# Between two transformer layers: zeros of two operand stacks written by ScalarE, the first head chunk of layer 1 placed by token half, its first maxima ordered by query tile

## The chip, the cores and the metric

One core of one Trainium2 chip. The metric is the device time of one execution in microseconds (us), lower is better. Engines are named as in the profile: PE (TensorE matmul), PEld (its weight loads), DVE (VectorE), ACT (ScalarE), POOL (GpSimd), SP (SyncE, which here only issues DMAs; SPq is its queue).

## The reference, cut to what matters

A two-layer block network over 1024 tokens (a 32 x 32 grid) of 384 channels, everything in float32:

```
x = x + attention0(ln(x))      # 12 heads of 32, full 1024 x 1024, relative positions
t = t + moe0(ln(t))            # 8 experts, 2 per token
x = x + attention1(ln(x))      # 12 query heads, 4 key/value heads, 7 x 7 neighbourhood
t = t + moe1(ln(t))            # 8 experts, 2 per token, and one shared expert
```

The change lies at the seam: the end of `moe0`, where each token gathers its two expert rows and adds them, and the start of `attention1`. In `attention1` the scores are `q k / sqrt(32)` inside the 7 x 7 window, a softmax over the window, and the weighted sum of values.

## The kernel before, in words

**Tiling.** The tokens stand in 8 tiles of 128 (`NT`), two halves of 4 tiles (`HALF`, 512 tokens each). The 12 query heads stand in 3 chunks of 4 (`KC` chunks, `G` heads). One core runs both layers in turn; each engine has its own program (`@block.sync`, `gpsimd`, `scalar`, `vector`, `tensor`), and they meet only in semaphores.

**End of layer 0.** The routed experts work on 23 blocks of 128 rows. When the last block's result is copied out of PSUM (`y_dve` reaches `ROUTED_BLOCKS`) SP stores it to DRAM (L602). POOL then gathers two rows per token, one tile at a time: 16 indirect DMAs (L880), two per tile, the tiles 4 to 7 only after the tile four (one less) before them has been added. DVE adds the two rows with their weights (L1367, L1369) and takes the statistics of the next layer norm (L1114). After four tiles DVE and ACT normalise the half (ACT's square root is L893), and PE transposes it (L1422).

**Start of layer 1.** PE transposes half 0, runs the four projection jobs of half 0 (keys, then the queries of the three chunks; L1397), transposes half 1 and runs the same four jobs for half 1. Each job is rounded by ACT into a high part (L923, L932) and its remainder taken by DVE as a low part (L1135), which raises `job_dve`. ACT and DVE copy the transposes of half 1 before they take the first job of half 0, because that is their program order.

**The stacks.** A score matmul contracts over 128 partitions: for each head the operand `QA` (queries) holds 32 rows of the high query part, 64 rows of mask, and the high part again; `KS` (keys) holds high keys, 64 rows of position keys and low keys; `QB` holds low queries, 32 rows that later take the row maxima, and 64 rows of zeros (partitions 64 to 127). The stacks of layer 1 lie in memory that layer 0's expert weights used, so they can be written only when the experts are done, except for `QA` and `KS` of stack 0, whose mask and position rows are placed during the experts. SP places `QA` and `QB` rows by SBUF-to-SBUF DMAs (`place`, L543), one per head and 32 rows; POOL places the keys (L777). Before, SP issued at the end of layer 0 three transfers of 1 MB each out of DRAM: zeros for `QB` of stack 0, mask for `QA` of stack 1, zeros for `QB` of stack 1. Then it waited for chunk 0's queries of both halves:

```
sp.wait_ge(job_dve, job_number(1, "q", 0))
stack_direct(0)                      # 8 DMAs into QA, 4 into QB, 128 KB each
sp.wait_ge(job_dve, job_number(1, "q", 2))
stack_direct(1)                      # the same for chunk 1
```

**First maxima.** The softmax subtracts a row maximum that is found ahead of the scores: PE makes the high-part scores of one head and one query tile (`max_piece`, L1471), DVE reduces them (L1156). The work goes in six blocks, chunk by chunk, half by half. The first block has 16 pieces (4 heads x the 4 query tiles of half 0), and nothing to run beside it but the 8 value projections (L1451), one after each second piece. A query tile needs the keys of its own tile and of one on each side. `tile_of` sets the order: head by head, four query tiles each. PE turns the maxima into rows (`maxima_rows`, L1485), ACT copies them into `QB` (`copy_rows`, L946), and the scores (L1501, L1503), exponentials (L962) and weighted sums (L1520, L1531) follow. The pieces of block n+1 go between the scores of block n. PE waited for all of `QA` of chunk 0 and all keys before the first piece:

```
pe.wait_ge(a_in[0], placed(A_DMAS, layer, 0))
pe.wait_ge(k_in[layer], 16 * K_DMAS)
for i in range(TILES):
    max_piece(first_block, i)
```

Of the kernel before, what the change touches and what calls it, by code (L numbers as in the profile page):

```python
# [41 lines left out]
P = 128  # L42
# [55 lines left out]
def build(nc, x, qkv_w, qk_b, v_b, proj_w, proj_b, rel_both, Wr0, br0, Wgu0, bgu0, Wd0, bd0,  # L98
# [17 lines left out]
    with ctx:  # L116
        def sem(name):
            return ctx.enter_context(nc.semaphore(name))
# [137 lines left out]
        zero_rows = nc.dram_tensor("zero_rows", [2 * D, T], F32, kind="Internal").ap()  # L256
# [34 lines left out]
        k_stored = sem("k_stored")  # L291
        a_in = [sem("a_in0"), sem("a_in1")]
# [63 lines left out]
        A_DMAS = [[17, 7, 6], [10, 9, 8]]  # L356
        B_DMAS = [[16, 4, 4], [5, 5, 4]]
# [120 lines left out]

        def tile_of(hb, j):

            return hb // HALF % KC, j // (NT // HALF), hb % HALF * (NT // HALF) + j % (NT // HALF)
# [37 lines left out]
        def _(sp):  # L519
# [37 lines left out]
            def place_same(dst, rows, done):  # L557

                place(dst, rows.rearrange("p (a t) -> p a t", a=1).broadcast_to([rows.shape[0], G, T]), done)
# [85 lines left out]
            for n in range(2):  # L645
                sp.dma_start(zero_rows[D * n:D * n + D, :], mask_const[0:D, :]).then_inc(const_stored, 16)
# [12 lines left out]
            sp.wait_ge(const_stored, 16 * 6)  # L659
            sp.wait_ge(proj_dve, NT)  # L660
            sp.dma_start(Wqkv[1][:, :, :], w_qkv1.rearrange("(k p) n -> p k n", p=P)).then_inc(wq_in[1], 16)
            place_same(KS[1][0][D:3 * D], key_rows[1], a_in[0])
            place_same(QA[1][0][D:3 * D], mask_rows, a_in[0])
            routed(0)

            place_same(QB[1][0][2 * D:P], zero_rows, b_in[0])
            place_same(QA[1][1][D:3 * D], mask_rows, a_in[1])
            place_same(QB[1][1][2 * D:P], zero_rows, b_in[1])
# [8 lines left out]
            sp.wait_ge(job_dve, job_number(1, "q", 0))  # L677
            stack_direct(0)
            check(a_in[0], A_DMAS[1][0])
            check(b_in[0], B_DMAS[1][0])  # L680
            sp.wait_ge(job_dve, job_number(1, "q", 2))
# [19 lines left out]
        def _(pool):  # L701
# [58 lines left out]
            for layer in range(2):  # L760
# [11 lines left out]
                if layer:  # L772

                    pool.wait_ge(job_dve, job_number(1, "k", 0))
                    for dst, src in ((KS[1][0][0:D], k_part(1, 0, False)), (KS[1][0][3 * D:P], k_part(1, 0, True))):
                        for g in range(G):
                            pool.dma_start(dst[:, g, :].bitcast(F32), src[D * g:D * g + D].bitcast(F32)).then_inc(k_in[1], 16)  # L777
# [108 lines left out]
        def _(act):  # L886
# [22 lines left out]
            for layer in range(2):  # L909
                ln_and_transposes(2 * layer)  # L910
# [27 lines left out]
                def copy_rows(c, half, pair):  # L938

                    hb = BLOCKS * layer + HALF * c + half  # L940
                    if pair == 0:
                        act.wait_ge(nmax_psum, hb + 1)
                        act.wait_ge(b_in[c % 2], placed(B_DMAS, layer, c))
                    rows = 1 if layer == 0 else D
                    for g in (2 * pair, 2 * pair + 1):
                        last = act.activation(QB[layer][c % 2][D:D + rows, g, half * BANK:(half + 1) * BANK],  # L946
                                              PS[D * g:D * g + rows, 4, :], ACT.Copy)
                    last.then_inc(nmax_act, 1)
# [431 lines left out]
        def _(pe):  # L1380
# [55 lines left out]
            for layer in range(2):  # L1436
# [116 lines left out]
                pe.wait_ge(a_in[0], placed(A_DMAS, layer, 0))  # L1553
                pe.wait_ge(k_in[layer], 16 * K_DMAS)
                first_block = BLOCKS * layer
                for i in range(TILES):
                    max_piece(first_block, i)
                    if i % 2 == 1:
                        values(i // 2)
# [6 lines left out]
                for c in range(KC):  # L1566
                    for u in range(U[layer]):
# [5 lines left out]
                        if some and some[0] == 0 and half == 1:  # L1573
                            pe.wait_ge(a_in[(c + 1) % 2], placed(A_DMAS, layer, c + 1))

# [174 lines left out]
```

## Time and profile before

| what | value |
|---|---|
| three runs | 1140.9, 1142.8, 1146.92 us, median 1142.8 |
| the profiled execution | 1143.17 us, of which the traced span is 1141.6 us |
| mean granted TensorE clock | 0.958 of full speed |
| busy share of the span | PE 89%, PEld 51%, DVE 45%, ACT 28%, POOL 28% |
| the seam, from the last expert store to the first score of layer 1 | 538.6 to 611.4 us of the span |

Times in rows are microseconds from the start of the span, ns where that is written. A timeline row is: start, duration, engine, line, operation, what is written and read, count, and in brackets the idle time of the engine ahead of it with what ended it. A row of several instructions (xN) is merged. Full speed of the clock is 2.4 GHz, its other level 1.2 GHz.

### The profile page before, as it was taken

To read this page: it belongs to the slowest core of one execution; us is meant where nothing else is said; L and a number is where in the kernel's file an instruction comes from. 1 tells how busy PE (TensorE), PEld (TensorE's weight loads), DVE (VectorE), ACT (ScalarE), POOL (GpSimd) and SP (SyncE) were. 2 spreads that over 40 slices of the span, in tenths; PEclk is the share of its full clock that TensorE was granted. 3 is DMA by queue.
4 is the path that set the end of the run, shared out by engine and by line. 5 is a ranking of instruction groups with operands and counts; after the bars stand their busy time and mean duration, and the time that the engine had idled before them with its cause. 6 is when DMAs were issued, how large, how long until landed. Compare 5 with 4: busy or idle time off the path is not lost.

```text
span 1141.6 us, 13662 instructions
## 1 busy us (share of the span) xinstructions
PE 1011.7 (89%) x4561; PEld 587.9 (51%) x4562; DVE 510.3 (45%) x898; ACT 321.9 (28%) x492; POOL 323.9 (28%) x281
## 2 busy tenths in 40 slices
PE   6999999999980799997278888979999999999998
PEld 3755555554440466664136656558554554455554
DVE  4566687888562255553534465671111111111114
ACT  3514544554611122121014545241111111111100
POOL 5514677777735001000510000254000000000004
PEclk9999999999995799999598999999999999999999
DMA  8599308000077236411733100523344424411005
GB/s 293 148 284 279 85 14 172 1 1 1 2 269 260 70 138 221 152 55 50 206 96 73 43 15 2 193 78 118 131 152 160 158 81 175 175 51 42 14 27 159
DMA packets 47114, 132.45 MB, mean 116 GB/s; under 512 B 6865, under 2 KB 25817, under 8 KB 46808
## 3 DMA queue, kind: packets, MB, share of 16 engines
q1 hardware_dynamic: 32424, 67.41, 20.4%
q0 software_dynamic: 14640, 64.36, 15.8%
q8 instruction: 32, 0.52, 0.2%
q14 instruction: 18, 0.15, 0.0%
HBM read 89.88 MB, written 30.87 MB: 106 GB/s over the span
## 4 chain that ended last, share of the span: by engine, by line
PE 71%; DVE 9%; DMA 8%; ACT 5%; issue 4%; POOL 3%; SPq 1%; POOLq 0%; DVEq 0%; ACTq 0%
PE PS L1667 21%; PE PS L1688 10%; PE PS L1471 6%; PE PS L1520 5%; PE PS L1397 5%; PE PS L1640 4%; DMA Wd<-in_Wd_r 4%; PE PS L1501 3%; DVE nmax_part L1156 3%; PE PS L1503 3%; PE PS L1714 3%; ACT QB L946 2%; DMA bd<-in_bd 2%; PE PS L1451 2%; DVE exp_acc L1188 2%
## 5 line engine op out<-in xcount | busy, mean ns | idle before, releaser
L1667 PE MATMUL PS<-Wgu,xbT 128*128 x690 | 285.5, 556 | 9.2 <-DMA Wd<-in_Wd_r 5.4
L1667 PEld LDWEIGHTS PS<-Wgu,xbT 128*128 128x128 f32 x690 | 127.9, 191 | 127.6 <-issue 114.8
L962 ACT ACTIVATE expS<-PS 128x1024 f32<-128x1024 f32 (+3 forms) x156 | 135.5, 878 | 135.2 <-PE PS L1503 134.0
L1688 PE MATMUL PS<-Wd,hidT 128*128 x414 | 143.1, 491 | 1.5 <-DVE hidT L1297 0.8
L798 POOL TENSOR_TENSOR exp_acc<-exp_acc,expS 128x512 f32<-128x512 f32 (+1 forms) x65 | 124.5, 1915 | 47.6 <-ACT expS L962 46.8
L1471 PE MATMUL PS<-KS,QA 128*128 128x512 f32 (+2 forms) x288 | 109.3, 426 | 18.7 <-DVE nmax L1156 6.8
L1501 PE MATMUL PS<-QA,KS 128*128 128x512 f32 (+3 forms) x312 | 116.9, 380 | 9.0 <-ACT QB L946 9.0
L1156 DVE TENSOR_REDUCE nmax_part<-PS 128x1 f32<-128x512 f32 x160 | 103.6, 684 | 46.0 <-PE PS L1471 45.2
L1503 PE MATMUL PS<-QB,KS 128*128 128x512 f32 (+3 forms) x312 | 111.7, 364 | 0.0
L1688 PEld LDWEIGHTS PS<-Wd,hidT 128*128 128x128 f32 x414 | 78.7, 191 | 57.6 <-issue 14.4
L1471 PEld LDWEIGHTS PS<-KS,QA 128*128 128x128 f32 x288 | 52.2, 191 | 83.1 <-DVE nmax_part L1156 44.6
L1071 ACT ACTIVATE hidT<-PS 128x384 f32<-128x384 f32 x46 | 22.6, 491 | 253.2 <-PE PS L1676 253.2
L1156 DVE TENSOR_REDUCE nmax<-PS 128x1 f32<-128x384 f32 (+2 forms) x112 | 66.4, 621 | 59.1 <-PE PS L1471 57.9
L880 POOL DMA_INDIRECT got<-block_rows_out,row_i x32 | 30.8, 963 | 211.7 <-DMA block_rows_out<-yb 199.8
L1501 PEld LDWEIGHTS PS<-QA,KS 128*128 128x128 f32 x312 | 59.9, 192 | 39.8 <-ACT QB L946 18.2
L1520 PE MATMUL PS<-expS,V 128*32 128x512 f32 (+3 forms) x624 | 71.6, 531 | 0.1
L1297 DVE COPY hidT<-PS 128x384 f32<-128x384 f32 x23 | 12.8, 558 | 120.1 <-PE PS L1676 120.0
L1503 PEld LDWEIGHTS PS<-QB,KS 128*128 128x128 f32 x312 | 60.1, 193 | 7.3
L1397 PE MATMUL PS<-XnT,Wqkv 128*128 128x512 f32 x120 | 56.9, 634 | 3.4 <-issue 2.0
L826 POOL DMA_DIRECT2D Wgu<-in_Wg_r x8 | 6.0, 755 | 189.2 <-DVE yb L1335 167.0
L1306 DVE TENSOR_TENSOR hid<-gated,PS 128x768 f32<-128x768 f32 x23 | 21.9, 954 | 79.8 <-ACT gated L1063 79.8
L1313 DVE TENSOR_TENSOR pre<-PS,bgu 128x768 f32<-128x768 f32 x23 | 22.0, 957 | 78.9 <-PE PS L1667 72.8
(170 smaller groups left out, 1177.2 us busy)
## 6 DMA issues: line engine op xcount, KB each, us to landing
Wgu<-in_Wgu POOLq DMA_DIRECT2D x8, 1152.0 KB, 6.3
Wgu<-in_Wg_r POOLq DMA_DIRECT2D x8, 1152.0 KB, 6.4
Wgu<-in_Wu_r POOLq DMA_DIRECT2D x8, 1152.0 KB, 8.5
Wd<-in_Wd_r POOLq DMA_DIRECT2D x8, 1152.0 KB, 10.8
xb<-block_rows_in SPq DMA_DIRECT2D x46, 192.0 KB, 2.4
block_rows_out<-yb SPq DMA_DIRECT2D x46, 192.0 KB, 1.9
part_rows<-parts SPq DMA_DIRECT2D x2, 3072.0 KB, 17.9
Wd<-in_Wd POOLq DMA_DIRECT2D x8, 576.0 KB, 7.1
```

The source lines that it names most:

```text
L798: last = pool.tensor_tensor(acc, older, exp_tile(0, c, u)[:, pair, heads], ALU.add)
L962: act.activation(exp_tile(layer, c, unit)[:, pair, :].rearrange("p (b n) -> p b n", b=2)[:, :, lo:hi], PS[:, 2 * pair:2 * pair + 2, lo:hi] ...
L1156: dve.tensor_reduce(dst, src, axis=AX.XY if hb == 0 else AX.X, op=ALU.max, negate=True).then_inc(max_done, 1)
L1397: last = pe.matmul(PS[:, bank, :], Wqkv[layer][:, kc, col:col + P], XnT[:, kc, b * BANK:(b + 1) * BANK], start=kc == 0, stop=kc == KC - 1)
L1471: last = pe.matmul(PS[:, bank + (k - lo) // BANK, 0:n], QA[layer][c % 2][:, g, qt * P:(qt + 1) * P], KS[layer][c % 2][:, g, k:k + n], star ...
L1501: pe.matmul(PS[:, 2 * pair + j, lo:hi], keys, QA[layer][c % 2][:, g, queries], start=True, stop=False)
L1503: last = pe.matmul(PS[:, 2 * pair + j, lo:hi], keys, QB[layer][c % 2][:, g, queries], start=False, stop=True)
L1520: last = pe.matmul(PS[D * g:D * g + D, 6, lo:hi], V[:, kt, vcol:vcol + D], probabilities(c, u, g), start=first, stop=last_one, skip_group_ ...
L1640: last = pe.matmul(PS[:, 2 * (n % 3) + up, :], w, rows, start=i == 0, stop=i == len(products) - 1)
L1667: last = pe.matmul(PS[:, 3 * par + lo // BANK, 0:n], xbT[:, par, kc, :], Wgu[layer][:, bass.ds(s, 1), kc, lo:lo + n], start=kc == 0, stop= ...
L1688: last = pe.matmul(PS[:, 7, 0:C], hidT[layer][:, par, i, :], Wd[layer][:, bass.ds(s, 1), i, :], start=i == 0, stop=i == m.IC - 1)
L1714: last = pe.matmul(PS[:, 3 + t % 3, 0:C], shared_hidT[:, f, t * P:(t + 1) * P], shared_d[:, f, :], start=f == 0, stop=f == m.IC - 1)
```

## The change

ScalarE writes the zero rows of both `QB` stacks, as soon as the last expert block is copied out, with two activations of 64 x 4096 elements (`Copy`, scale 0). The two 1 MB zero loads, their DRAM tensor and the two stores that filled it go away. The 1 MB mask load for `QA` of stack 1 is issued by SP after chunk 0's queries. Chunk 0's queries and the keys are placed in two token halves, so with twice as many DMAs of half the size (64 KB): half 0 when the first two jobs (SP) or the first job (POOL) are done, half 1 after jobs 6 and 5. The first block's pieces go query tile by query tile, four heads each; the first 12 need only half 0, the last 4 also the keys of half 1. PE waits for the early semaphores in front of the first piece, for half 1's keys in front of piece 12, and for half 1's queries in front of the second block's first piece. ACT waits for the early `QB` rows in front of the first `copy_rows`.

```diff
--- before.py
+++ after.py
@@ -253,7 +253,6 @@
         ys = nc.dram_tensor("block_rows_out", [ROUTED_BLOCKS * P, C], F32, kind="Internal").ap()
 
         key_rows = [nc.dram_tensor(f"key_rows{n}", [2 * D, T], F32, kind="Internal").ap() for n in range(2)]
-        zero_rows = nc.dram_tensor("zero_rows", [2 * D, T], F32, kind="Internal").ap()
         mask_rows = nc.dram_tensor("mask_rows", [2 * D, T], F32, kind="Internal").ap()
 
 
@@ -289,6 +288,10 @@
         hi_act = sem("hi_act")
         parts_stored = sem("parts_stored")
         k_stored = sem("k_stored")
+        a_early = sem("a_early")
+        b_early = sem("b_early")
+        k_early = sem("k_early")
+        fixed_in = sem("fixed_in")
         a_in = [sem("a_in0"), sem("a_in1")]
         b_in = [sem("b_in0"), sem("b_in1")]
         v_psum = sem("v_psum")
@@ -353,8 +356,8 @@
         block = ctx.enter_context(nc.Block())
 
 
-        A_DMAS = [[17, 7, 6], [10, 9, 8]]
-        B_DMAS = [[16, 4, 4], [5, 5, 4]]
+        A_DMAS = [[17, 7, 6], [8, 9, 8]]
+        B_DMAS = [[16, 4, 4], [4, 4, 4]]
 
         W_LOAD = [16 * 4, 16 * 3]
         W_BEFORE = [0, E * W_LOAD[0]]
@@ -476,8 +479,12 @@
 
             return (BLOCKS - 1 + TAIL_CUTS) * (hb // BLOCKS) + hb % BLOCKS
 
+        EARLY_TILES = (NT // HALF - 1) * G
+
         def tile_of(hb, j):
 
+            if hb == BLOCKS:
+                return 0, j % G, j // G
             return hb // HALF % KC, j // (NT // HALF), hb % HALF * (NT // HALF) + j % (NT // HALF)
 
         def piece_place(hb, i):
@@ -642,8 +649,6 @@
 
             sp.wait_ge(pool_const, 3)
             sp.dma_start(mask_rows[:, :], mask_const[D:3 * D, :]).then_inc(const_stored, 16)
-            for n in range(2):
-                sp.dma_start(zero_rows[D * n:D * n + D, :], mask_const[0:D, :]).then_inc(const_stored, 16)
 
             sp.wait_ge(k_stored, 16 * 2)
             sp.wait_ge(parts_stored, 16 * PARTS_STORED)
@@ -656,16 +661,12 @@
             stack_from_rows(2)
 
 
-            sp.wait_ge(const_stored, 16 * 6)
+            sp.wait_ge(const_stored, 16 * 4)
             sp.wait_ge(proj_dve, NT)
             sp.dma_start(Wqkv[1][:, :, :], w_qkv1.rearrange("(k p) n -> p k n", p=P)).then_inc(wq_in[1], 16)
-            place_same(KS[1][0][D:3 * D], key_rows[1], a_in[0])
-            place_same(QA[1][0][D:3 * D], mask_rows, a_in[0])
+            place_same(KS[1][0][D:3 * D], key_rows[1], fixed_in)
+            place_same(QA[1][0][D:3 * D], mask_rows, fixed_in)
             routed(0)
-
-            place_same(QB[1][0][2 * D:P], zero_rows, b_in[0])
-            place_same(QA[1][1][D:3 * D], mask_rows, a_in[1])
-            place_same(QB[1][1][2 * D:P], zero_rows, b_in[1])
 
             def stack_direct(c):
 
@@ -674,10 +675,21 @@
                     place_direct(QA[1][s][lo:lo + D], q_part(1, c, False), "qk", a_in[s])
                 place_direct(QB[1][s][0:D], q_part(1, c, True), "qk", b_in[s])
 
-            sp.wait_ge(job_dve, job_number(1, "q", 0))
-            stack_direct(0)
+            for half in range(HALF):
+                cols = slice(half * BANK, (half + 1) * BANK)
+                done_a, done_b = (a_early, b_early) if half == 0 else (a_in[0], b_in[0])
+                sp.wait_ge(job_dve, JOBS[0] + JOBS[1] // HALF * half + 2)
+                for lo in (0, D * 3):
+                    for g in range(G):
+                        place(QA[1][0][lo:lo + D, g, cols], q_part(1, 0, False)[D * g:D * g + D, cols].bitcast(F32), done_a)
+                for g in range(G):
+                    place(QB[1][0][0:D, g, cols], q_part(1, 0, True)[D * g:D * g + D, cols].bitcast(F32), done_b)
+            check(fixed_in, 2)
+            check(a_early, 2 * G)
+            check(b_early, G)
             check(a_in[0], A_DMAS[1][0])
             check(b_in[0], B_DMAS[1][0])
+            place_same(QA[1][1][D:3 * D], mask_rows, a_in[1])
             sp.wait_ge(job_dve, job_number(1, "q", 2))
             stack_direct(1)
             check(a_in[1], A_DMAS[1][1])
@@ -771,10 +783,13 @@
 
                 if layer:
 
-                    pool.wait_ge(job_dve, job_number(1, "k", 0))
-                    for dst, src in ((KS[1][0][0:D], k_part(1, 0, False)), (KS[1][0][3 * D:P], k_part(1, 0, True))):
-                        for g in range(G):
-                            pool.dma_start(dst[:, g, :].bitcast(F32), src[D * g:D * g + D].bitcast(F32)).then_inc(k_in[1], 16)
+                    for half in range(HALF):
+                        cols = slice(half * BANK, (half + 1) * BANK)
+                        pool.wait_ge(job_dve, JOBS[0] + JOBS[1] // HALF * half + 1)
+                        for dst, src in ((KS[1][0][0:D], k_part(1, 0, False)), (KS[1][0][3 * D:P], k_part(1, 0, True))):
+                            for g in range(G):
+                                pool.dma_start(dst[:, g, cols].bitcast(F32),
+                                               src[D * g:D * g + D, cols].bitcast(F32)).then_inc(k_in[1] if half else k_early, 16)
 
                 def accumulate(hb, v):
 
@@ -907,6 +922,12 @@
                 copy(1, 0)
 
             for layer in range(2):
+                if layer:
+
+                    act.wait_ge(y_dve, ROUTED_BLOCKS)
+                    for low in QB[1]:
+                        act.activation(low[2 * D:P, :, :].rearrange("p g t -> p (g t)"),
+                                       ones[2 * D:P, 0:1].broadcast_to([2 * D, G * T]), ACT.Copy, scale=0.0)
                 ln_and_transposes(2 * layer)
                 if layer == 0:
                     act.wait_ge(qk_bias_in, 16)
@@ -940,7 +961,10 @@
                     hb = BLOCKS * layer + HALF * c + half
                     if pair == 0:
                         act.wait_ge(nmax_psum, hb + 1)
-                        act.wait_ge(b_in[c % 2], placed(B_DMAS, layer, c))
+                        if hb == BLOCKS:
+                            act.wait_ge(b_early, 16 * G)
+                        else:
+                            act.wait_ge(b_in[c % 2], placed(B_DMAS, layer, c))
                     rows = 1 if layer == 0 else D
                     for g in (2 * pair, 2 * pair + 1):
                         last = act.activation(QB[layer][c % 2][D:D + rows, g, half * BANK:(half + 1) * BANK],
@@ -1550,10 +1574,16 @@
                     last.then_inc(sums_psum, 1)
 
 
-                pe.wait_ge(a_in[0], placed(A_DMAS, layer, 0))
-                pe.wait_ge(k_in[layer], 16 * K_DMAS)
+                if layer:
+                    pe.wait_ge(fixed_in, 16 * 2)
+                    pe.wait_ge(a_early, 16 * 2 * G)
+                    pe.wait_ge(k_early, 16 * K_DMAS)
                 first_block = BLOCKS * layer
                 for i in range(TILES):
+                    if layer == 0 and i == 0:
+                        pe.wait_ge(a_in[0], placed(A_DMAS, 0, 0))
+                    if i == (EARLY_TILES if layer else 0):
+                        pe.wait_ge(k_in[layer], 16 * K_DMAS)
                     max_piece(first_block, i)
                     if i % 2 == 1:
                         values(i // 2)
@@ -1572,6 +1602,8 @@
                         per = 2 if layer == 0 else 1
                         if some and some[0] == 0 and half == 1:
                             pe.wait_ge(a_in[(c + 1) % 2], placed(A_DMAS, layer, c + 1))
+                        if some and some[0] == 0 and layer and c == half == 0:
+                            pe.wait_ge(a_in[0], placed(A_DMAS, 1, 0))
 
 
                         after = (c, u + 1) if u + 1 < U[layer] else (c + 1, 0)
```

## Rows read from the trace of the kernel before

**Rows 1.** Chain of waits over the whole span, shares by engine (the page, part 4)

```profile
PE 71%; DVE 9%; DMA 8%; ACT 5%; issue 4%; POOL 3%; SPq 1%; POOLq 0%; DVEq 0%; ACTq 0%
```

**Rows 2.** Chain of waits, 536 to 615 us: start, duration, what

```profile
547.01 9.94 DMA got<-block_rows_out,row_i
...
562.33 3.36 PE PS L1422 x12
...
566.36 13.21 PE PS L1397 x24
...
591.01 1.48 SPq L543
...
594.47 3.36 DMA QA<-q_part
...
608.62 1.28 ACT L987
...
610.12 0.59 ACT QB L946
```

**Rows 3.** Timeline, 537 to 562 us

```profile
538.94 0.66 SPq L543 DMA_DIRECT2D QB<-zero_rows  x1
...
549.51 0.95 POOL L880 DMA_INDIRECT got<-block_rows_out,row_i  x1 [0.30 <-issue]
...
558.76 0.60 DVE L1367 SCALAR_TENSOR_TENSOR X<-got,weight,X 128x384 f32<-128x384 f32 x1
...
561.26 0.20 ACT L893 ACTIVATE std<-var_eps 128x4 f32<-128x4 f32 x1 [26.28 <-DVE var_eps L1099]
```

**Rows 4.** The one gather (L880) that starts in 558 to 559 us

```profile
L880 POOL DMA_INDIRECT got<-block_rows_out,row_i x1: 947/947/947, 558.5 to 558.5; - x1
...
DMA to landing us min/median/max: 3.1/3.1/3.1
```

**Rows 5.** The 16 gathers of layer 1 (L880, 1110 to 1130 us), issue to landing

```profile
DMA to landing us min/median/max: 2.9/3.6/4.6
```

**Rows 6.** The three 1 MB transfers (L543, 535 to 545 us), issue to landing

```profile
DMA to landing us min/median/max: 7.7/11.0/17.5
```

**Rows 7.** Busy time in stretches: length, engines' busy (count), PE clock, DMA share, GB/s

```profile
544.00:550.00 6.00, 0.00 (x0) 0.00 (x0) 0.00 (x0) 0.00 (x0) 4.48 (x6) 0.50 1.01 325
...
566.30:571.60 5.30, 5.24 (x6) 2.18 (x7) 4.76 (x14) 0.21 (x2) 0.00 (x0) 0.50 0.01 3
...
592.40:598.00 5.60, 0.01 (x1) 0.00 (x0) 0.69 (x1) 0.60 (x1) 0.00 (x0) 0.79 0.92 244
598.00:602.50 4.50, 4.43 (x19) 4.47 (x20) 2.02 (x5) 0.56 (x2) 0.00 (x0) 0.51 0.93 203
...
612.50:616.10 3.60, 3.52 (x13) 3.52 (x13) 0.56 (x1) 2.04 (x4) 0.00 (x0) 0.53 0.02 5
```

**Rows 8.** ScalarE by shape: the longest plain activation

```profile
L962 ACT ACTIVATE expS<-PS 128x1024 f32<-128x1024 f32 x96 | 97.7, 1026 | 86.9 <-PE PS L1503 86.6
```

**Rows 9.** Timeline, 580 to 600 us: low parts of the jobs and placements

```profile
582.29 1.87 DVE L1135 SCALAR_TENSOR_TENSOR q_part<-PS,q_part 128x512 fp32r<-128x512 f32 x3
...
586.34 4.01 POOL L777 DMA_DIRECT2D KS<-k_part  x8 [22.78 <-DVE k_part L1135]
...
588.65 6.41 SPq L543 DMA_DIRECT2D QA<-q_part  x8
...
593.08 0.69 DVE L1135 SCALAR_TENSOR_TENSOR q_part<-PS,q_part 128x512 fp32r<-128x512 f32 x1 [1.88 <-ACT q_part L923]
```

**Rows 10.** The reductions of the first block (L1156, 590 to 612 us)

```profile
L1156 DVE TENSOR_REDUCE nmax<-PS x16: 424/547/558, 598.7 to 607.9; 128x1 f32<-128x384 f32 x12, 128x1 f32<-128x256 f32 x4
```

**Rows 11.** Timeline of PE: first piece, maxima rows of block 1, first piece of chunk 1

```profile
598.07 0.87 PE L1471 MATMUL PS<-KS,QA 128*128 128x256 f32 x2 [5.65 <-DMA QA<-q_part]
...
608.55 1.08 PE L1485 MATMUL PS<-ident,nmax 128*32 128x128 f32 x32 [0.27 <-DVE nmax L1156]
...
634.40 0.28 PE L1471 MATMUL PS<-KS,QA 128*128 128x256 f32 x1
```


## The prediction

> **What bounds the kernel now.** I read the page's chain first: PE carries 71% of it and DMA 8% [rows 1], so time off PE is worth looking for only where PE stands still. The chain between 536 and 615 us shows two such places at the seam.
>
> *Place A, the combine.* Before PE can transpose half 0 of layer 1's input at 562.33, the chain sits 9.94 us in one gather that POOL issued at 547.01 [rows 2]. The timeline shows what else was in flight: SP issued the first of its three 1 MB transfers at 538.94, just ahead of the gathers [rows 3]. They took 7.7 to 17.5 us to land [rows 6], and in 544 to 550 the DMA engines were busy for the whole stretch (share 1.01) while no compute engine but POOL, which issues the gathers, did anything [rows 7]. A gather issued at 558.5, when the three had landed, took 3.1 us [rows 4]; the 16 gathers of layer 1, without such company, took 2.9 to 4.6 [rows 5].
>
> *Place B, the placement.* The last low part of the jobs ends at 593.08 + 0.69 = 593.77 [rows 9]. The first piece of the maxima starts at 598.07, and what it waited for is a `QA` placement [rows 11]. In the chain that is SP's issues, one after the other, and 3.36 us of landing [rows 2]. Then PE's granted clock is at its lower level (0.51) for 598 to 602.5, after a stretch in which PE had done almost nothing [rows 7].
>
> After the seam everything hangs on PE's progress through layer 1: its loads and its stages are released by the attention's own steps, so what is gained ahead of the first scores should reach the end whole.
>
> **Part 1: zeros by ScalarE.** It removes two of the three transfers ahead of the gathers; moving the mask (part 2) removes the third. The last gather of half 0 is the eighth, issued at 549.51 [rows 3]; nothing in its issue waits for DVE, so that time stays. It lands after 3.1 us [rows 4] instead of being served behind 3 MB: 549.51 + 3.1 = 552.6, and the fourth tile's addition, which started at 558.76 [rows 3], starts there: **6.15 us** earlier. (The third tile, issued at 547.01, would be landed by 550.1 and added in time.) From there statistics, normalisation and PE's transposes follow as before: 562.33 becomes 556.2. Bounds: 2.9 and 4.6 us of landing [rows 5] give 6.35 and 4.65.
>
> Half 1 does not become the new bound. POOL no longer waits for DVE, so the sixteenth gather is issued some 8 x 1.25 us after the eighth (POOL's pace between 547.01 and 549.51 [rows 2, 3]), at 559.5, and lands by 562.7; with the 3.6 us from addition to transpose that half 0 takes (558.76 to 562.33), half 1 is ready at 566.3. PE is busy with half 0's jobs until 556.2 plus what it needs now from 562.33 to 579.57 (566.36 + 13.21) [rows 2], so until 573.4: 7 us of cover.
>
> The price on ScalarE: 1024 elements per partition take 1.03 us [rows 8], so 4096 take at most 4.1 and two of them 8.2, from about 538.9 (SP's zero load waits for the same last block [rows 3]) to 547.1. Its next work is the square root, due at 561.26 - 6.15 = 555.1, idle 26 us before it [rows 3]. So they cost nothing, with 8 us of cover, even if a table load of 1.28 us [rows 2] comes behind them. If the cover were gone, each us would delay half 0's normalisation by as much.
>
> PE starts half 0's jobs at the clock's lower level now (0.50 from 566.3 to 571.6 [rows 7]). It has still stood idle for some 18 us before, so I leave that as it is. Reaching the full clock a us sooner or later would be worth about 0.5 us, up or down.
>
> **Part 2: placement by half, and the mask moved.** In this part I keep the trace's own times, without the 6.15. The first two jobs' low parts are there at 582.29 + 1.87/3 = 582.9 [rows 9]. SP then issues eight early `QA` DMAs. Eight took 6.41 us, two long ones among them [rows 9, 2], so the eighth is issued by 588.7 and, with the old landing of 3.36 for twice the bytes, is there at 592.1. POOL's eight early key DMAs take 4.01 us of issue [rows 9]; from 582.9 they are out at 586.9 and, with the slowest landing of rows 5, there by 591.5. Both are ahead of 593.77, when the last low part is ready and PE, which waits for all eight jobs, may go on. So PE's wait changes owner: no longer a DMA, but DVE's last low part. First piece at about **594.0** instead of 598.07: 4.05 us. Cover: 1.7 us; a later landing costs what exceeds it.
>
> Half 1's keys, eight more POOL issues, are out by 591 and there by 595.5; piece 12 comes no sooner than 599. Half 1's queries are the twentieth SP issue: 582.9 + 20 x 0.80 (6.41/8) = 598.9, landing 602.3. PE wants them after the first scores, which wait for ACT's row copies (610.12 now [rows 2], about 604.4 then): 2 us of cover at that slow pace. Behind them in SP's queue stand four `QB` DMAs, the mask and chunk 1's twelve, treated under the rivals.
>
> **Part 3: order of the pieces.** The 16 reductions are the same, 12 x 0.558 + 4 x 0.424 = 8.4 us of DVE [rows 10]. PE's gap in front of them shrinks from 4.3 us to its own wait for DVE, some 1.6 us, so I expect its clock to stay at full speed, and then DVE's rate is the bound: 594.0 + 0.35 to the first output + 8.4 = 602.75, where the rows start at 608.55 today [rows 11]. That is **5.75 us** in all for place B. If the clock falls as it does now, the pace of today stays and B is worth 4.05 (the lower bound). Above it: if the second slow stretch, 612.5 to 616.1 at 0.53 [rows 7], goes as well, half of its 3.6 us, 1.8 more. ACT's table load and row copies follow the last value copy as now and shift with it.
>
> The two dropped stores early in layer 0 and the new semaphore waits have cover of many us and I cost them at nothing.
>
> **Sum.** 6.15 + 5.75 = 11.9 us. The profiled execution took 1143.17 around its span of 1141.6, 0.4 above the median of the three runs; 1143.17 - 11.9 = 1131.3, from the median 1130.9. I say **1131**. The terms' bounds give 4.65 + 4.05 = 8.7 (1134.3) to 6.35 + 5.75 + 1.8 = 13.9 (1129), and with the runs' scatter 1127 to 1135 for this case alone. From no change such a measurement can tell about 0.5%, 5.7 us.
>
> **Rivals.**
> *Only the gathers gain.* The early placement is late or something else holds the first piece: 1143.17 - 6.15 = 1137.0. For it: when POOL and SP placed together, some SP issues took up to 1.48 us [rows 2], and the cover is 1.7 us. Against: half the bytes per DMA. Chance 0.09.
>
> *Only the placement gains.* The gathers are slow by themselves: 1137.4. Against it stand the 3.1 us of a gather after the transfers [rows 4] and layer 1's [rows 5]. Chance 0.05.
>
> *More DMAs eat the gain.* SP issues 24 placements for chunk 0 instead of 12. At 1.48 us each, half 1's queries would land at 582.9 + 29.6 + 3.4 = 615.9, 11.5 late, and nothing is left: 1142.8. Only two issues of the old twelve were so long. Chance 0.07 for this or a like loss.
> The Trainium skill ("DMA: Bandwidth & Descriptors", rules for kernel authors) speaks against this part: it says to coalesce many small transfers, because under 64 KB mostly overhead is paid, and gives about 2 us plus bytes over 436 GB/s for one. By that an estimate is 2.15 us for 64 KB against 2.3 for 128; were the eight early ones served one after another, they would be done at 600.1, B would lose 2 us instead of gaining, and the time would be about 1139. The trace does not agree that they are serial: eight of 128 KB were out in 6.41 us and the last landed 3.36 us after its issue [rows 9, 2].
>
> *Slower: chunk 1 comes late.* The mask, 1 MB, now stands in SP's queue between chunk 0's 24 and chunk 1's 12 placements, and PE wants chunk 1 at 634.40 [rows 11], 628.65 with B's gain. 37 issues at 0.80 end at 612.5; with the slowest landing of a 1 MB transfer, 17.5 [rows 6], that is 630, a loss of 1.4 us only. At 1.1 us per issue with that landing it is 641 and the gain is gone; at 1.25 it is 646.7, 18 late, and the time is 1149. Against: the mask has no other 1 MB transfers and no gathers beside it there. Chance 0.03.
>
> **How the numbers follow.** The forecast has 0.76. The range has to reach to the two half gains, so 1127 to 1137.5. Faster by over 0.5%: 0.76, the 0.09 (6.15 is just over 5.7) and half of the 0.05, so 0.88. Within 0.5%: the rest of that and the 0.07, so 0.09. Slower: 0.03.
>
> **What the changed profile would show.** The gathers L880 of half 0 land in about 3 us and the DMA share ahead of them is well under 1; two ScalarE activations of some 4 us begin right after the last expert block. The chain at the seam goes through POOL's gather issues, not through a 9.9 us DMA. The first piece is released by the last DVE low part, some 0.2 us after it; the clock in that stretch stays near 1. No wait of PE on half 1's queries or on chunk 1. Wrong would be: gathers of 7 us or more; a first piece released by a DMA; a clock of 0.5 under the first maxima; or a gain at the first score that is smaller at the end of the attention.

## The result and the profile after

The changed kernel takes 1135.15 us (median of 8 runs, 1130.58 to 1136.01) against 1143.27 for the kernel before (8 runs, 1140.9 to 1148.52): ratio 0.9911, 95% interval 0.9889 to 0.9933. A second batch of the same kernel gave 1133.27 and the same ratio. 1143.27 x 0.0089 is 10.2 us less, with the interval 7.7 to 12.7; the medians themselves lie 8.1 us apart, in the second batch 9.8. The forecast was 11.9, inside the interval. The profiled execution took 1133.86 us around a span of 1132.3.

The chain of waits of the changed kernel, down to the row copies, answers to [rows 2] (start, duration, what); the last three lines are from later stages:

```profile
550.12 3.00 DMA got<-block_rows_out,row_i
...
556.68 3.37 PE PS L1446 x12
...
560.73 13.04 PE PS L1421 x24
...
587.27 0.70 DVE q_part L1159
...
588.42 0.47 PE PS L1495 x2
...
596.93 1.28 ACT L1011
...
598.44 0.59 ACT QB L970
...
728.55 4.32 PE PS L1455 x6
...
861.65 11.12 DMA Wd<-in_Wd_r
...
872.95 7.08 PE PS L1699 x12
```

The 9.94 us in one gather have become 3.00, the `QA` placement and SP's issues are gone from the chain, and in their place stands DVE's last low part (the line that is left out between the last low part and the first piece is 0.45 us of issue). The first row copy comes at 598.44 instead of 610.12, although the layer before it ended 0.6 us later here (the first gather starts at 541.27 instead of 540.67).

The timeline of the combine answers to [rows 3]; the brackets say how long the engine had been idle and what ended that:

```profile
539.18 7.12 ACT L929 ACTIVATE QB<-ones 64x4096 fp32r<-64x4096 f32 x2 [4.80 <-DVE yb L1361]
...
546.31 1.28 ACT L908 ACT_TABLE_LOAD   x1
...
553.14 0.62 DVE L1391 SCALAR_TENSOR_TENSOR X<-got,weight,X 128x384 f32<-128x384 f32 x1 [0.60 <-DMA got<-block_rows_out,row_i]
...
555.70 0.20 ACT L908 ACTIVATE std<-var_eps 128x4 f32<-128x4 f32 x1 [8.11 <-DVE var_eps L1123]
```

Two zero activations take 7.1 us, 3.6 each, and 8.1 us of cover (idle time of ScalarE before its square root) are left. In 544 to 550 us the DMA share is 0.58 where it was 1.01 [rows 7]. All 16 gathers land in about 3 us now (min, median, max; 3.0, 7.5 and 9.9 before):

```profile
L895 POOL DMA_INDIRECT got<-block_rows_out,row_i x16: 942/946/1316, 541.3 to 560.7; - x16
...
DMA to landing us min/median/max: 3.0/3.0/3.7
```

Around the first maxima the busy time in stretches answers to [rows 7] (length, busy time of PE, PEld, DVE, ACT, POOL, PE clock, DMA share, GB/s). PE's gap is 1.8 us, and the clock stays:

```profile
586.60:588.40 1.80, 0.00 (x0) 0.01 (x1) 0.69 (x1) 0.60 (x1) 0.00 (x0) 1.00 0.44 114
588.40:590.40 2.00, 1.98 (x17) 2.00 (x18) 1.44 (x4) 0.28 (x1) 0.00 (x0) 1.00 0.40 98
590.40:592.40 2.00, 2.00 (x18) 2.00 (x17) 1.79 (x5) 0.56 (x2) 0.00 (x0) 1.00 0.40 98
```

**What the end gets.** The span is 9.3 us shorter, the first row copy 12.3 nearer to the first gather, and the start of layer 1's output projection 12.8 nearer. So the gain came through the attention whole, and some of it went behind it. The last lines of the chain show where, beside the same work in the kernel before (the router's six matmuls, and the expert block after the second wait for weights):

```profile
740.74 2.74 PE PS L1431 x6
...
883.62 5.41 PE PS L1667 x12
```

In the changed kernel part of both ran at the clock's lower level: the mean granted clock is 0.63 in 728.4 to 733.0 and 0.76 in 873.0 to 880.1, and it was 1.00 for both in the kernel before. Whether the change does that, or chance, is what several of the experiments below were also made for.

### The profile page after: what moved, and what is told of

Its sections match the earlier page's. It is cut to its first block, busy times and chain, and to the rows that moved or that the text cites. A ratio compares the mean times of both kernels' runs of the same rounds, so it can differ in the third digit from the quotient of the medians.

```text
span 1132.3 us, 13681 instructions
## 1 busy us (share of the span) xinstructions
PE 1011.8 (89%) x4561; PEld 585.7 (52%) x4562; DVE 510.7 (45%) x898; ACT 328.9 (29%) x494; POOL 328.3 (29%) x289
## 4 chain that ended last, share of the span: by engine, by line
PE 72%; DVE 9%; DMA 7%; ACT 5%; issue 4%; POOL 3%; POOLq 0%; DVEq 0%; SPq 0%; ACTq 0%
PE PS L1699 22%; PE PS L1720 10%; PE PS L1495 5%; PE PS L1421 5%; PE PS L1544 5%; PE PS L1672 4%; DMA Wd<-in_Wd_r 4%; PE PS L1525 3%; DVE nmax_part L1180 3%; PE PS L1527 3%; PE PS L1746 3%; ACT QB L970 2%; DMA bd<-in_bd 2%; PE PS L1475 2%; PE PS L1708 2%
## 5 line engine op out<-in xcount | busy, mean ns | idle before, releaser
L1720 PEld LDWEIGHTS PS<-Wd,hidT 128*128 128x128 f32 x414 | 78.7, 191 | 57.5 <-issue 14.1
L1495 PEld LDWEIGHTS PS<-KS,QA 128*128 128x128 f32 x288 | 51.5, 188 | 79.0 <-DVE nmax_part L1180 44.5
L1321 DVE COPY hidT<-PS 128x384 f32<-128x384 f32 x23 | 12.8, 557 | 122.5 <-PE PS L1708 122.4
```

Source lines behind the costliest of these rows:

```text
L1495: last = pe.matmul(PS[:, bank + (k - lo) // BANK, 0:n], QA[layer][c % 2][:, g, qt * P:(qt + 1) * P], KS[layer][c % 2][:, g, k:k + n], star ...
L1720: last = pe.matmul(PS[:, 7, 0:C], hidT[layer][:, par, i, :], Wd[layer][:, bass.ds(s, 1), i, :], start=i == 0, stop=i == m.IC - 1)
```

## The experiments

All ratios are against runs of the kernel before on the same chip. Layer 0 ends up to 5 us earlier or later from profile to profile, so the table counts from the start of the first gather. Columns: first transpose of half 0, first piece of the maxima, first row copy; then the stretch from layer 1's output projection to the end, and the span.

| profile | transpose | piece | row copy | projection to end | span |
|---|---|---|---|---|---|
| before | 21.6 | 57.4 | 69.4 | 420.1 | 1141.6 |
| before, `b0_copy` | 22.2 | 57.4 | 69.4 | 423.0 | 1147.2 |
| before, `b1_copy` | 21.4 | 54.4 | 66.5 | 420.9 | 1141.4 |
| before, `b2_copy` | 21.3 | 56.8 | 69.2 | 420.9 | 1141.7 |
| changed | 15.4 | 47.1 | 57.2 | 423.0 | 1132.3 |
| changed, `a0_copy` | 15.4 | 47.3 | 59.0 | 421.1 | 1131.9 |
| `e1_zeros_by_dma` | 20.7 | 51.5 | 61.5 | 423.7 | 1138.1 |
| `e2_mask_early` | 15.5 | 47.5 | 57.5 | 422.9 | 1132.7 |
| `e3_part1_only` | 15.6 | 50.9 | 62.9 | 422.6 | 1139.1 |
| `e3_again` | 15.4 | 50.8 | 62.9 | 423.7 | 1141.0 |
| `e4_old_order` | 15.4 | 46.9 | 57.0 | 423.5 | 1134.3 |
| `e5_zeros_three_times` | 21.6 | 50.9 | 62.5 | 420.6 | 1137.0 |
| `v1_wait_by_bank` | 15.5 | 45.1 | 56.4 | 420.7 | 1128.1 |
| `v2_table_early` | 15.4 | 44.4 | 55.3 | 423.4 | 1128.4 |

**The changed kernel again** (`a0_copy`, no edit).

> The changed kernel as it is, once more, to see how much of it repeats. In the changed profile the seam gains 12.2 us by the start of the attention's output projection (709.3 against 721.5), but the span only 9.3: from that projection to the end it takes 423.0 us against 420.1 before, with the same instructions. Theory S (seam gain whole and steady, the later 2.9 us are chance in where PE's clock falls and in when weights land): the projection starts at 709.3 within 1 us again, the stretch from there to the end varies by 1 to 4 us from profile to profile and lies between 419 and 424. Rival G (the change itself makes the later stages slower): the stretch is 423 again within 0.5. Total 1131 to 1136 in both.

Measured: 1133.27 us (6 runs), ratio 0.9911 (0.9886 to 0.9935). The stretch to the end was 421.1, so it does vary; the router's matmuls took 2.74 us again, the block after the second weight wait 7.11. The projection started at 710.76, 1.4 later than in the first profile and just outside what was expected, because the seam itself was 1.8 us longer: here the clock did fall after the same 1.8 us gap. (It fell in `e5_zeros_three_times` as well, to 0.60 in 594.0 to 596.5; in `e1_zeros_by_dma`, `e2_mask_early` and `e4_old_order` it stayed at 1.00 from the first piece to the maxima rows.)

```profile
585.70:587.50 1.80, 0.02 (x1) 0.00 (x0) 0.69 (x1) 0.60 (x1) 0.00 (x0) 1.00 0.43 115
587.50:589.50 2.00, 1.96 (x15) 1.99 (x16) 1.42 (x4) 0.28 (x1) 0.00 (x0) 0.87 0.40 98
589.50:591.50 2.00, 2.00 (x10) 2.00 (x10) 1.12 (x3) 0.28 (x1) 0.00 (x0) 0.50 0.40 98
```

The three stretches answer to the three of the first profile above; in the last one PE does 10 matmuls in the time of 18.

**Zeros by DMA again, the rest as changed.**

```diff
   routed(0)
+  place_same(QB[1][0][2 * D:P], zero_rows, b_early)
+  place_same(QB[1][1][2 * D:P], zero_rows, b_in[1])
   ...
-  for low in QB[1]:
-      act.activation(low[2 * D:P, :, :].rearrange("p g t -> p (g t)"), ..., ACT.Copy, scale=0.0)
```

The DRAM tensor of zeros and the stores that fill it come back too.

> The changed kernel, but the zeros come by the two 1 MB DMAs out of DRAM again, issued ahead of the gathers; the mask stays behind chunk 0. Theory (gathers wait behind the bytes in the DMA engines, 1 MB per some 3.1 us at the 325 GB/s of the trace): 2 MB ahead, so the gathers of half 0 land in 6 to 7.5 us instead of 3, the fourth tile's addition 3 to 4 us later than in the changed kernel, total 3 to 4.5 us more. Rival (any large transfer beside them slows the gathers to the old 8 to 10 us): 6 us more. Second rival (gathers slow by themselves): no difference from the changed kernel.

Measured: 1138.05 us, ratio 0.9948 (0.9929 to 0.9967); by the ratios 4.2 us more than the changed kernel, inside the 3 to 4.5 expected. But the transposes came 5.3 us later, not 3 to 4; the first piece is only 4.2 to 4.4 later than in the two profiles of the changed kernel, so the total fits although the step in front of it does not. The two zero loads and the eight gathers of half 0, issue to landing:

```profile
L551 SPq DMA_DIRECT2D QB<-zero_rows x2: 616/639/662, 541.1 to 541.8; - x2
...
DMA to landing us min/median/max: 7.6/10.3/13.0
```

```profile
L900 POOL DMA_INDIRECT got<-block_rows_out,row_i x8: 942/946/996, 542.8 to 551.6; - x8
...
DMA to landing us min/median/max: 5.7/8.5/10.3
```

The second load was in at 541.8 + 13.0 = 554.8; the first gather landed at 552.8, the eighth, issued at 551.6, at 557.3. So 2 MB cost nearly what 3 MB did. My rate was the error: 3.1 us per MB is the 325 GB/s that the engines moved in the kernel before with the gathers counted in [rows 7]. Here they were as busy (share 1.03 in 546 to 552) and moved 219 GB/s, and the two zero loads were both in 13.0 us after the second was issued. Why the rate is lower here stays open.

**Mask ahead of the gathers again.**

```diff
   routed(0)
+  place_same(QA[1][1][D:3 * D], mask_rows, a_in[1])
   ...
   check(b_in[0], B_DMAS[1][0])                          # chunk 0 is placed
-  place_same(QA[1][1][D:3 * D], mask_rows, a_in[1])
```

> The changed kernel, but the 1 MB mask load stands ahead of the gathers again. Theory of bytes: 1 MB is out of the way by 545, the first two or three gathers land late, the eighth in 3 to 4 us; addition of the fourth tile 0 to 1 us later, total 0 to 1 us more. Rival (any large transfer beside them): 4 to 6 us more.

Measured: 1134.32 us, ratio 0.9919 (0.9894 to 0.9943). The load landed in 5.2 us; the first gather took 4.0 instead of 3.1, the eighth 3.0:

```profile
L550 SPq DMA_DIRECT2D QA<-mask_rows x1: 580/580/580, 539.5 to 539.5; - x1
...
DMA to landing us min/median/max: 5.2/5.2/5.2
```

So moving the mask is worth nothing that shows. What freed the gathers is that the two zero loads are gone. These runs don't tell whether any two loads of 1 MB would do the same harm; one of them, the mask, does not.

**Part 1 alone** on the kernel before: zeros by ScalarE, mask behind chunk 0, placement and order of before; run twice.

> The kernel before with part 1 alone: zeros by ScalarE, mask behind chunk 0, whole placement of chunk 0, old order. Theory: the combine gains its 6.15 us, the placement nothing: the output projection starts 6 us earlier than in the kernel before (715.4), total 6 us less than before. Rival (the placement does not matter once the gathers are free): as the changed kernel, 10 to 12 less.

> Part 1 alone, a second profile. Its first profile gains 6.5 us at the seam, yet its runs are only 2.5 us faster in the mean than the kernel before. Theory S (the seam's gain is steady, and the total scatters with where PE's clock falls, which moves with the phase that the clock's changes have in a run): the row copies again 62.9 us after the first gather within 0.7, and the time at the lower clock over the span differs from the first profile's by several us. Rival: the seam itself scatters by several us (row copies at 66 or later).

Measured: 1140.17 us (12 runs), ratio 0.9978 (0.9962 to 0.9994), so 2.5 us, 0.7 to 4.3. The transposes gain the whole 6 us, the row copies stand at 62.9 in both profiles, and the chain ends in the old placement wait:

```profile
551.18 3.08 DMA got<-block_rows_out,row_i
...
589.68 3.30 DMA QA<-q_part
...
593.22 0.88 PE PS L1472 x2
```

The seam behaves as forecast, the total gains less than half of the 6 us expected; see below. The second profile (its own time is 1142.56 us) was expected to spend several us more or less at the lower clock than the first; it did not, the mean granted clock is 0.960 in both.

**Old order of the pieces**, the rest as changed.

```diff
-  EARLY_TILES = (NT // HALF - 1) * G
+  EARLY_TILES = NT // HALF - 1
   ...
-  if hb == BLOCKS:
-      return 0, j % G, j // G
```

> The changed kernel with the first maxima head by head again; chunk 0 stays placed by half, and PE waits for the keys of half 1 in front of piece 3 instead of 12. Theory (the order has nothing to wait for any more: in the changed profile POOL's last key DMA is issued at 584.8 and lands some 3 us later, before PE may start the first piece at 588.4): first piece and row copies as in the changed kernel within 0.5 us, total the same within 0.3%. Rival (the order is what lets the maxima start early, as the diff puts it): first maxima stand still at piece 3, row copies 1 to 3 us later.

Measured: 1134.87 us, ratio 0.9921 (0.9902 to 0.994); row copies at 57.0 against 57.2. The order is worth nothing here: half 1's keys land (1.9 to 2.5 us after POOL's last issue, which starts at 584.3 in the changed profile) before PE may start any piece. Against part 1 alone, which has the old order too, the row copies are 5.9 us earlier: that is what the placement by halves is worth by itself.

**Six zero activations instead of two.**

```diff
+  for extra in (QB[1][0][0:2 * D], QB[1][1][0:2 * D], QA[1][1][0:2 * D], QA[1][1][2 * D:P]):
+      act.activation(extra.rearrange("p g t -> p (g t)"), ..., ACT.Copy, scale=0.0)
```

> The changed kernel with six zero activations instead of two: four more of the same size into rows that are overwritten later. In the changed profile two take 7.1 us, the square root's table load 1.3, and ScalarE then waits 8.1 us for the statistics. Theory (cover of 8.1 us, beyond it one for one): 14.2 us more work, 14.2 - 8.1 = 6.1 us later from the square root on, total 6 us more. Rival (ScalarE's writes also slow the gathers or DVE): more than 7.

Measured: one time, 1138.62 us, 3.5 and 5.4 above the two medians of the changed kernel where 6 was expected. ScalarE is late by the forecast amount:

```profile
554.38 7.22 ACT L932 ACTIVATE QA<-ones 64x4096 fp32r<-64x4096 f32 x2
561.60 1.28 ACT L908 ACT_TABLE_LOAD   x1
562.90 0.20 ACT L908 ACTIVATE std<-var_eps 128x4 f32<-128x4 f32 x1
```

The transposes come at 21.6, 6.2 us later. The gathers still land in 3.0 to 3.4, so ScalarE's writes do not slow them. But the first piece is only 3.8 us later: PE's clock rose sooner after the transposes (see the profiles of the kernel before, below).

**The kernel before, three more profiles** (no edit).

> The kernel before as it is, once more. From the output projection of layer 1 to the end its profile took 420.1 us; the changed kernel and its four variants took 421.1 to 423.7. They differ by PE's clock under the router's matmuls (4.3 us against 2.7) and under the expert block after the second wait for weights (7.1 against 5.4), and in how long that wait is. Theory S (chance): this second profile of the kernel before lies among the others, 421 to 424, with one or both of the slow stretches. Rival G (the change makes the later stages slower): 420 again, both stretches at full clock.

> The kernel before, a third profile. The stretch from the output projection of layer 1 to the end was 420.1 and 423.0 in its first two. Theory S: somewhere in 420 to 424. Rival G (the changed kernel's 421.1 to 423.0 are its own): 420 in most.

> The kernel before, a fourth profile, for the same question and with the same two expectations: 420 to 424 if it is chance, 420 if the later stages of the changed kernel are slower by themselves.

Measured, projection to end: 423.0, 420.9, 420.9 beside the first profile's 420.1. `b0_copy` has the slow block after the second weight wait too:

```profile
875.89 10.81 DMA Wd<-in_Wd_r
...
886.88 7.11 PE PS L1667 x12
```

In `b1_copy` the seam was 3 us shorter than in the others. The reason is in its stretches, beside those of the first profile of before: PE's first transpose is at 564.1 there and 562.3 here.

```profile
564.10:567.40 3.30, 3.29 (x12) 2.33 (x12) 3.23 (x7) 1.20 (x2) 1.16 (x1) 0.50 0.46 126
567.40:575.00 7.60, 6.91 (x17) 3.15 (x17) 7.01 (x19) 0.80 (x2) 0.00 (x0) 1.00 0.01 3
```

```profile
562.30:565.60 3.30, 3.27 (x12) 2.33 (x12) 3.23 (x7) 1.20 (x2) 1.16 (x1) 0.50 0.44 124
565.60:571.70 6.10, 5.41 (x8) 2.24 (x8) 5.51 (x16) 0.80 (x2) 0.00 (x0) 0.50 0.02 4
571.70:575.00 3.30, 3.30 (x9) 1.50 (x8) 1.56 (x4) 0.00 (x0) 0.00 (x0) 1.00 0.00 0
```

The same work, and the full clock comes 3.3 us after the first transpose in the one and 9.4 in the other. (In `e5_zeros_three_times` it was early as well.)

**Two versions beyond the change.** The first lets PE wait for the bank that a piece takes instead of all eight jobs; the second also loads the exponential table ahead of the value copies.

```diff
-  for n in range(njobs - 8, njobs):      # now in layer 0 alone
-      evacuated(pe, layer, n)
   ...
+  if layer and i < 3:                    # in front of piece i of layer 1
+      evacuated(pe, 1, 2 * i + 2)
```

```diff
+  act.activation(warm[:, :], ones[:, 0:1], ACT.Exp)    # ahead of the copies into V
   ...
-  act.activation(warm[:, :], ones[:, 0:1], ACT.Exp)    # behind them
```

> The changed kernel, where PE no longer waits for all eight jobs in front of layer 1's first piece but, piece by piece, for the job whose PSUM bank the piece takes. Theory (PE's 1.8 us gap there is DVE's last low part and nothing else, the early queries and keys have landed by 585.5): the first piece starts within 0.3 us of PE's last job, 1.5 to 1.8 us earlier; DVE starts its reductions right after the last low part, 0.8 us earlier; and with no gap the clock does not fall under the maxima, as it did in the copy of the changed kernel (0.50 for about 3 us, row copies 1.7 us later) and not in the first profile of it. Row copies 0.5 to 1 us earlier than in the changed profile's best case (relative to the first gather 56.3 to 56.8 against 57.1 and 59.0), total 1 to 2 us less. Rival (a placement lands later than thought): the first piece is released by a DMA.

> The version with the waits by bank, and ScalarE's exponential table is loaded ahead of the value copies instead of behind the last one, in both layers. In the traces so far that load (1.28 us) and the small activation behind it stand between the last value copy and the first row copy: at the seam the row copies start 0.4 to 0.5 us after the maxima rows are done, in layer 0 about as much or a little more. Theory: first row copy of layer 1 at 55.8 to 56.1 us after the first gather (56.4 without it), 0.8 to 1.4 us less in total than the version with the waits alone. Rival (PE's rows were last anyway): no difference.

Measured: 1132.32 us, ratio 0.9902 (0.9881 to 0.9922), and 1128.9 us, ratio 0.9874 (0.9852 to 0.9897). With the waits by bank the first piece comes 2.0 us earlier and the row copies 0.8 before the better profile of the changed kernel, both about as expected. With the table early they gain another 1.1, more than the 0.3 to 0.6 expected; ScalarE is no longer last, it waits 1.1 us for the rows:

```profile
592.49 1.08 PE L1509 MATMUL PS<-ident,nmax 128*32 128x128 f32 x32 [0.27 <-DVE nmax L1179]
593.64 2.41 ACT L970 ACTIVATE QB<-PS 32x512 fp32r<-32x512 f32 x4 [1.10 <-PE PS L1509]
```

By the ratios the second version is 3.2 us faster than the first, where 0.8 to 1.4 was expected; their intervals overlap, and since the table moves in layer 0 too, which the table above does not count, the seam is not all of it. The second version beats the kernel before clearly. Against the changed kernel its interval overlaps by a hair (0.9897 and 0.9889, or 0.9886 for the second batch); every one of its 5 runs (1127.53 to 1130.57) is faster than all but one of the 14 of the changed kernel. The second version ran on another chip than the second batch of the changed kernel, so that comparison is not a clean one.

## Why the prediction was right, and where it was off

**Place A, 6.15 us: right.** The four profiles of before transpose at 21.3 to 22.2 after the first gather, the changed ones at 15.4: 6.2 in the mean. The gather lands in 3.0, half 1 is no bound, ScalarE's zeros have 8.1 us of cover, and the run with six of them shows that beyond the cover each us counts. That I had said 8 is luck: the zeros were 1.1 us shorter than I took them, and the table load, which I had not taken off, uses 1.3. Another detail was wrong as well: the cause is the two zero loads, and the mask, the third transfer in my sum, adds nothing that shows.

**Place B, 5.75 us: the mechanism right, the size at one or the other of my two values.** PE's first piece is released by DVE's last low part, as forecast, 0.46 us behind it where I had said 0.2. The cleanest measure is part 1 alone, which has the new place A and the old place B: its row copies stand at 62.9. Against it the first profile of the changed kernel gains 5.7 us and its copy 3.9; the two variants that keep the placement by halves, `e2_mask_early` and `e4_old_order`, gain 5.4 and 5.9. The step "I expect its clock to stay at full speed" holds in one profile of the changed kernel and fails in its copy, which is then near my lower bound of 4.05. Over all six profiles with PE's 1.8 us gap the clock stayed up in four and fell in two. In the two versions that wait by bank, where PE's first piece follows its last job at once, the granted clock was 1.00 under the maxima in the one profile of each. Two slips in my working change nothing: 608.55 - 602.75 is 5.8, and PE's own gap in the kernel before was 5.65 us [rows 11], not the 4.3 from the last low part on.

**The order and the mask: not priced apart.** I put the order of the pieces and the moved mask into the terms without a price of their own; alone, each is worth nothing measurable. The halves are what place B needs, since with the old order they alone give 5.9 us.

**"What is gained ahead of the first scores should reach the end whole": to the end of the attention it does, to the end of the kernel not quite.** With all profiles, the row copies stand at 68.6 in the mean of four for the kernel before and 58.1 in the mean of two for the changed one: 10.5 us. The stretch to the end is 421.2 and 422.1, 0.8 the other way. Together that is 9.7, against 10.2 measured. So of the 2.2 us between 9.7 and the forecast 11.9, some 1.4 are missing at the row copies already (the clock that fell in one of the two profiles, and a baseline of mine with one of the longest seams of the four), and 0.8 behind the attention. The forecast lies inside the measured interval, so the runs alone do not show that the point was too low.

For part 1 alone the same reckoning gives 68.6 - 62.9 = 5.7 less 423.2 - 421.2 = 2.0, so 3.7; measured were 2.5 (0.7 to 4.3). So 6 us at a seam need not be 6 us at the end. Part of the difference are stretches at the lower clock after waits: the router's matmuls (+1.6) in four of the eight profiles that have the new placement and in none of the other six; the block after the second weight wait (+1.7) in one of the four of before, one of the two of part 1 alone and six of the eight with the new placement. In `e3_again` and `e4_old_order` another block was slow instead, 256 us after the start of the projection (7.11 us for 5.41). So one expert block was slow in one of four profiles of before and in nine of the ten others, all but `v1_wait_by_bank`. These stretches don't make up the whole: `e3_again` has one of them, +1.7, and yet a stretch to the end that is 2.5 above the mean of before. The stretch was 420.1 to 423.0 in the kernel before and 420.6 to 423.7 in all the others, so much of it is scatter. That moving the seam raises its mean by about a us is possible and not settled by so few profiles; the cause is open.

**The rivals.** Neither half gain came alone. More DMAs did not eat anything: SP's eight early `QA` issues took 4.5 us to the start of the last, none was long, and they landed in 2.0 to 2.8 instead of 3.36, half 0's queries complete by 584.5 and the last low part done at 588.0. The Trainium skill ("DMA: Bandwidth & Descriptors", rules for kernel authors) says to coalesce many small transfers, which speaks against the split; the trace shows no loss from it, since twice the transfers cost only queue time that was free. The fit that the prediction took from the Trainium skill stands in another section of that page ("Anatomy of one DMA", for transfers issued by GpSimd); its 2.15 us for 64 KB is near what the trace shows (1.9 to 2.5 for POOL's keys, 2.0 to 2.8 for SP's queries), and the loss worked out from it does not come because the transfers overlap. No wait for half 1's queries or for chunk 1 appears among PE's waits.

## What to carry to other kernels

When small gathers stand on the critical path, look at what large transfers another queue has just issued, and at whether an idle engine can make those bytes instead: the zeros cost ScalarE 7.1 us that were free where their loads cost the chain 5.3. Test each part of such a change alone, since here two of its four pieces did nothing. And a gain at one place is to be read in several profiles: a clock that comes back early, or falls after a wait, moved single profiles here by up to 3 us at one place, half of what either place gained.

## What was not expected of the hardware

The gathers did not share the DMA engines evenly with SP's loads. With 2 MB ahead, the first gather (128 rows of 384 floats) was issued 1 us after the second load and landed 10.0 us later, 2 us before that load; the other seven followed within 4.5 us. With 1 MB ahead it lost only 1 us. Two loads of 1 MB took 7.6 and 13.0 us; one with the gathers took 5.2, and the mask behind chunk 0's placements in the changed kernel 6.4.

PE's return to the full clock after nearly the same pause (24.6 and 24.3 us) and with the same work differed by 6 us between two profiles of one kernel (3.3 and 9.4 us after the first transpose), which was worth 3 us at the first piece.
